# A hypergraph layer whose 512-column rows are turned by VectorE and DMAs instead of TensorE

## The reference

```python
def hypergraph_conv(x, adj, W, b):
    H = (adj != 0).astype(x.dtype)
    w = adj.reshape(N, -1)[:, :C]                  # the first row of adj
    xw = jnp.einsum('ncd,hd->nch', x, W)
    Dn = jnp.einsum('nce,ne->nc', H, w)
    Dn = jnp.where(Dn > 0, 1.0 / Dn, 0.0)
    Be = H.sum(axis=1)
    Be = jnp.where(Be > 0, 1.0 / Be, 0.0)
    m = Be[:, :, None] * jnp.einsum('nce,nch->neh', H, xw)
    out = Dn[:, :, None] * jnp.einsum('nce,neh->nch', H, m)
    return out + b

h = jax.nn.relu(hypergraph_conv(x, adj, W1, b1))   # 512 columns
h = layer_norm(h, gamma, beta)
y = hypergraph_conv(h, adj, W2, b2)
return y + x
```

## Time and profile before

| | us |
|---|---|
| median of three runs | 2948.34 |
| the profiled execution | 2946.47 |
| its span, first to last instruction | 2944.7 |
| PE busy | 2819.0 |
| DVE busy | 1853.9 |
| ACT busy | 1485.6 |
| POOL busy | 723.1 |

### The profile page before, as it was taken

One profiled execution on the slowest core, in us unless ns is written; L12 is line 12 of the kernel. 1 busy time (PEld: TensorE's weight loads), 2 busy tenths in 40 slices (PEclk: granted clock), 3 DMA queues, 4 the chain that ended last, 5 costly groups with the idle time before them and its releaser, 6 DMA issues.

```text
span 2944.7 us, 61858 instructions
## 1 busy us (share of the span) xinstructions
PE 2819.0 (96%) x21760; PEld 2239.6 (76%) x21760; DVE 1853.9 (63%) x3994; ACT 1485.6 (50%) x2761; POOL 723.1 (25%) x1305
## 2 busy tenths in 40 slices
PE   8989999899998999989999999999999999999999
PEld 7777787787877878778687786877868778687786
DVE  3787427874288742887428864398643886439862
ACT  2883318833288332873228732387223872238622
POOL 0342003420034201342013420134101441014410
PEclk9999999999999999999999999999999999999999
DMA  5562215623166130661316613156122661126600
GB/s 177 186 196 93 91 61 194 200 81 113 47 202 209 57 135 35 204 216 42 131 50 196 214 50 118 67 189 219 57 96 79 190 219 64 74 82 198 199 8 15
DMA packets 210505, 371.89 MB, mean 126 GB/s; under 512 B 23312, under 2 KB 136336, under 8 KB 210192
## 3 DMA queue, kind: packets, MB, share of 16 engines
q1 hardware_dynamic: 208656, 363.59, 37.3%
q0 software_dynamic: 1536, 4.20, 0.4%
HBM read 220.64 MB, written 92.54 MB: 106 GB/s over the span
## 4 chain that ended last, share of the span: by engine, by line
PE 71%; DVE 15%; issue 7%; POOL 3%; ACT 2%; SPq 1%; DVEq 1%; DMA 0%; POOLq 0%; ACTq 0%
PE ps L1266 37%; PE ps L1432 7%; PE ps L1552 7%; PE ps L1489 7%; PE ps L1454 6%; PE ps L1627 4%; DVE junk L973 3%; POOL H L696 2%; DVE Z L929 2%; DVE stats L747 1%; SPq L507 1%; DVE h L989 1%; DVE dn L982 1%; DVE h L1007 1%; DVE Zx L929 1%
## 5 line engine op out<-in xcount | busy, mean ns | idle before, releaser
L1432 PE MATMUL ps<-kS,qS 128*128 128x512 f32 x1024 | 380.3, 454 | 88.3 <-DVE nm L929 85.9
L929 DVE CUSTOM_DVE_ANT_0 Z<-ps,adjN 128x1024 f32<-128x1024 f32 x328 | 393.7, 1207 | 36.1 <-PE ps L1432 34.8
L1187 ACT ACTIVATE Z<-Z,nm 128x1024 f32<-128x1024 f32 x328 | 378.2, 1156 | 18.0 <-POOL nm L684 16.9
L696 POOL TENSOR_SCALAR H<-adjN 128x128 fp32r<-128x128 f32 (+1 forms) x456 | 317.5, 697 | 0.0
L1177 ACT ACTIVATE PTa<-ps 128x512 f32<-128x512 f32 x464 | 253.9, 597 | 63.6 <-PE ps L1454 62.4
L1432 PEld LDWEIGHTS ps<-kS,qS 128*128 128x128 f32 x1024 | 161.0, 189 | 163.3 <-DVE nm L929 134.5
L684 POOL TENSOR_TENSOR nm<-nm,minus 128x1 f32<-128x1 f32 x512 | 98.2, 192 | 582.9 <-DVE nm L929 582.6
L1454 PEld LDWEIGHTS ps<-ident,Z 128*128 128x128 f32 x1792 | 204.7, 140 | 39.1 <-issue 14.8
L1454 PE MATMUL ps<-ident,Z 128*128 128x128 f32 x1792 | 233.4, 274 | 0.6
L929 DVE CUSTOM_DVE_ANT_0 Zx<-ps,adjN 128x1024 f32<-128x1024 f32 x184 | 221.0, 1204 | 8.0 <-PE ps L1432 6.9
L1266 PE MATMUL ps<-mh,adjT 128*128 128x256 f32 x1024 | 223.6, 379 | 0.8 <-issue 0.8
(11 more groups left out here) (192 smaller groups left out, 6202.7 us busy)
## 6 DMA issues: line engine op xcount, KB each, us to landing
blocks_kept<-blocks_in SPq DMA_DIRECT2D x160, 512.0 KB, 3.0
blocks_even<-blocks_kept SPq DMA_DIRECT2D x288, 128.0 KB, 3.4
adjT<-adjT_in SPq DMA_DIRECT2D x8, 4096.0 KB, 14.2
adjN<-adj_in SPq DMA_DIRECT2D x8, 4096.0 KB, 17.3
PTb<-blocks_kept SPq DMA_DIRECT2D x224, 128.0 KB, 3.5
PTz<-blocks_kept SPq DMA_DIRECT2D x128, 128.0 KB, 3.3
adjT<-adjT_in SPq DMA_DIRECT2D x8, 2048.0 KB, 7.7
qS<-qhi SPq DMA_DIRECT2D x112, 128.0 KB, 2.1
```

What stands on the lines that cost most here:

```text
L696: done = pool.tensor_scalar(H[:, t, of], adjN[:, t, of], 0.0, 0.0, ALU.is_equal, ALU.is_equal)
L929: dve.tensor_tensor_reduce(Z_of(u), ps[:, 2 * (u % 2):2 * (u % 2) + 2].rearrange("p a n -> p (a n)"), adjN[:, u // HEADS], SCORE_SCALE, LO ...
L1187: act.activation(Z_of(u), Z_of(u), ACT.Exp, bias=nm[:, u:u + 1], accum_out=sm[:, HEADS * (u // HEADS) + place(u):HEADS * (u // HEADS) + pl ...
L1432: mm = pe.matmul(ps[:, 2 * (u % 2) + s], qS[:, hd, rows(t)], kS[:, hd, half(s)], start=True, stop=True)
```

## The change

After the change DVE turns each tile of h2 in 32x32 blocks into a buffer `h2_turned` (two tiles), as soon as relu is done and ahead of the statistics. SP writes the buffer to DRAM (`h2_kept`); after each second tile it waits for both writes and reads both tiles back into `h2T` with four DMAs, one for each 32 partitions. Each DMA has 8 pieces of 512 bytes on each of 32 partitions. `h2T` has a new layout: the four blocks of columns of a row lie next to each other, so the elements of one stationary tile for x2 stand 16 bytes apart, and DVE writes its blocks with the same step. PE's transposes and ACT's copies go. The subtraction that makes Ul moves from DVE to POOL, between the scales of the third and the fourth norm.

```diff
@@ signals
-        h2T_ps = signal("h2T_ps", FT * NH)
-        h2Ts = signal("h2Ts", FT * NH)
+        h2_blocks = signal("h2_blocks", NT)
+        h2_out = [signal(f"h2_out{n}", 16 * (NT // 2)) for n in range(2)]
+        h2T_in = [signal(f"h2T_in{n}", 16 * QUADS) for n in range(NT // 2)]
@@ SP, after the loads of the weights
+                for t in range(NT):
+                    sp.wait_ge(*h2_blocks(b, t + 1))
+                    stand(sp, waited_sp)
+                    sp.dma_start(h2_kept[t], h2_turned[:, t % 2]).then_inc(h2_out[t % 2].sem, 16)
+                    if t % 2:
+                        for n in range(2):
+                            sp.wait_ge(*h2_out[n](b, 16 * (t // 2 + 1)))
+                            stand(sp, waited_sp)
+                        for to in range(QUADS):
+                            sp.dma_start(h2T[SQ * to:SQ * (to + 1), t - 1:t + 1].rearrange("p t (a q) f -> p (t a) (q f)", q=SQ),
+                                         h2_kept[t - 1:t + 1].rearrange("t (a p) c n -> p c (t a) n", p=SQ)[:, to]).then_inc(h2T_in[t // 2].sem, 16)
@@ POOL, batch()
                 norm_scale(b, 3)
+                for t in range(NT):
+                    pool.wait_ge(*x2h(b, t + 1))
+                    pool.tensor_tensor(Ul[:, t], h[:, t, 0:D], Uh[:, t].bitcast(F32), ALU.subtract).then_inc(x2s.sem, 1)
                 norm_scale(b, 4)
@@ DVE, the loop over y
                     if t:
                         dve.wait_ge(*yrelu(b, t))
+                        if t > 2:
+                            dve.wait_ge(*h2_out[(t - 1) % 2](b, 16 * ((t - 1) // 2)))
+                        dve.transpose(h2_turned[:, (t - 1) % 2].rearrange("p a (q c) -> p c a q", q=SQ), h2[:, t - 1]).then_inc(h2_blocks.sem, 1)
                         statistics(b, 3, t - 1, h2[:, t - 1])
@@ DVE, the loop over x2
-                    dve.wait_ge(*x2h(b, t + 1))
-                    dve.tensor_tensor(Ul[:, t], h[:, t, 0:D], Uh[:, t].bitcast(F32), ALU.subtract).then_inc(x2s.sem, 1)
@@ ACT
-                def copy_h2T(s):
...
-                    if t == H2T_AT - 1:
-                        copy_h2T(0)
...
-                    if t == TPH - 2:
-                        copy_h2T(1)
@@ PE
-                def transpose_h2(s):
...
-                    if t == H2T_AT:
-                        transpose_h2(0)
...
-                    if t == TPH - 2:
-                        transpose_h2(1)
-                    if t % TPH == 0:
-                        pe.wait_ge(*h2Ts(b, FT * (t // TPH + 1)))
+                    if t % 2 == 0:
+                        pe.wait_ge(*h2T_in[t // 2](b, 16 * QUADS))
...
-                    product(ps[:, t % 4, 0:D], [(h2T[:, f, rows(t)], W2g[:, f]) for f in range(FT)]).then_inc(x2_ps.sem, 1)
+                    product(ps[:, t % 4, 0:D], [(h2T[:, t, :, f], W2g[:, f]) for f in range(FT)]).then_inc(x2_ps.sem, 1)
```

More of the change, by code:

```diff
@@ L186, in build_program @@
              ("PTb", [P, PTS - PTA - 1, NT, P], F32), ("rs", [P, HEADS, HD], F32), ("Rs", [P, GROUPS, P], F32)],
-            [("h2", [P, NT, HID], F32), ("h2T", [P, FT, N], F32)],
+            [("h2", [P, NT, HID], F32), ("h2T", [P, NT, QUADS * SQ, FT], F32)],
             [("hh", [P, NT, HW], F32R), ("hl", [P, NT, D], F32R), ("wB", [P, N], F32), ("junk", [P, N], F32)],
@@ L191, in build_program @@
             [("padc", [P, NH, NT, HALF], F32), ("shiftB", [P, 2, D], F32),
-             ("b1B", [P, HID], F32)],
+             ("b1B", [P, HID], F32), ("h2_turned", [P, 2, QUADS, FT * SQ], F32)],
         )
@@ L200, in build_program @@
         P3, E3 = p3
-        _, shiftB, b1B = p2c
+        _, shiftB, b1B, h2_turned = p2c
+        h2_kept = nc.dram_tensor("h2_kept", [NT, P, QUADS, FT * SQ], F32, kind="Internal").ap()
         (r1, r2, r3) = region(
@@ L445, in weighed_before @@
             return GROUPS * (u // HEADS - 1) + place(u) // HPG + 1
-        H2T_AT = TPH + 2
         EARLY_EDGES = (5, 6, 4)
```

## The result

The changed kernel takes **3012.06 us** (median of four runs, 3010.18 to 3015.33) against 2948.2 before on the same chip: ratio 1.0215, 95% interval 1.0203 to 1.0228. The forecast was 2992, range 2955 to 3042: slower, as forecast, by 64 us instead of 44. The profiled executions differ by 66.1 us (span 3010.8 against 2944.7), 8.3 us a pass.

What follows compares the result with a forecast made beforehand. PE, busy 96%, bounds the kernel; after the change SP's round trip, 5.2 us per two tiles, does. Each pass loses 5.8 less 0.34, so 5.5 us; eight passes, 44 us, on 2946.5, plus 1.9, give 2992 us, range 2955 to 3042.

Steps and rivals of the forecast that it cites:

- the 0.34 us of the earlier trace: Edge sums: their wait for DVE's last x2 tiles goes, as no subtraction is left between those tiles; 0.34 us less a pass.
- PE needs 16 x 0.216 = 3.46 us for two tiles: x2 products: PE's time for each pair of tiles, 3.46 us, below SP's step of 5.2 us.
- Rival 2: PE slows while it waits for x2's reads: first pair alone costs nothing, all four pairs give 3077 us; chance 4%.
- Rival 1: x2's weight loads, slowed by the 16-byte step from 190 ns to 380, cost 5 us more a pass: 3032 us; chance 15%.
- I take no penalty: DVE's new block transposes: writing with a 16-byte step costs nothing extra, so each takes 0.70 us.
- SP's steps of 5.2, 5.45 and 5.2 us: SP's round trip per two tiles (four reads, two writes, waits): 5.2 us, the second step with 0.25 us of DVE's.
- Rival 3: The trip is short and PE's saving real: 13 us gained, 2935 us; chance of a gain 4%, of a tie 5%.
- DVE alone would pace: Were a pair in 4.0 us after its transpose, DVE would set the pace and the fourth pair start 1.3 us earlier.
- GpSimd's subtractions: Eight subtractions moved to GpSimd, about 0.65 us each, hidden behind the edge sums; without that cover they would cost 1 us.

Runs made afterwards that it cites:

- e7: The changed kernel with a few matmuls without use ahead of each pair's wait, so that PE does not stand still: 3000.43 us.
- e1: The changed kernel without the 16-byte step in DVE's blocks and in x2's weights (product mixes columns, only its time is of use): 3000.63 us.
- e2: The changed kernel with only the x2 weights lying side by side, DVE still writing with the 16-byte step (product not the reference's): 3010.94 us.
- e3: The changed kernel with only DVE writing in runs of 32 elements, the weights still with the 16-byte step (product not the reference's): 3006.44 us.
- e5: The changed kernel with x2 multiplying untransposed h2 without waiting for the trip, which still runs (not the reference's product): 2985.38 us.
- e6: e5 with DVE also writing its blocks in runs of 32 elements (not the reference's product): 2970.04 us.
- e4: The kernel before, with nothing but the subtraction moved to GpSimd: 2946.99 us, ratio 0.9996.
- e9: e8 with e1's two edits and matmuls without use, (3, 1, 1, 1), before the pairs: 2977.29 us, ratio 1.0097.
- e8: The changed kernel with the reads issued by ScalarE's queue, so that SP has only writes: 2993.81 us.

## Why the prediction was right, and its size too small

The mechanism was right: the new wait is the trip from DVE to DRAM and back, SP's round trip paces it, and nothing behind the edge sums gives the delay back but the 0.34 us of the earlier trace rows (from the sums to the next pass's y it is 331.7 us in the fourth pass, before 332.2). Its steps for the fourth pass, forecast and trace, in us from the start of y:

| | forecast | after |
|---|---|---|
| first, second reads issued | 13.4, 18.6 | 13.36, 18.83 |
| third, fourth reads issued | 24.0, 29.2 | 24.35, 30.01 |
| first pair starts | 18.6 | 17.92 |
| fourth pair starts | 34.5 | 35.28 |
| sums over edges start | 37.7 | 40.56 |

- **The step that failed: "PE needs 16 x 0.216 = 3.46 us for two tiles"**, used for the last pair as 3.27 until the sums. It takes 5.28: 2.0 of the 2.8 us that are missing in the fourth pass. 1.5 are the lower clock; e7 gives back 1.45. The other 0.5 it takes at the full clock as well: the last pair of e7 and of the changed kernel's first pass needs 3.75 instead of 3.27. With loads of 190 ns such a pair needs 3.37 (e1), so 0.4 of it is the weights' step and 0.1 the start behind a wait.
- **Rival 2** had the right mechanism with too few cases: the first pair alone (costs nothing) or all four (3077). The trace shows a third: the clock also falls behind the gap ahead of the *last* pair, and nothing is left there to hide it. I had put the later gaps at 1.7 us; the last is 2.45. The Trainium skill ("TensorE: Matmul & The Clock Gate", HAM oscillation — how this bites in real kernels) describes a low clock after each DMA wait that is longer than the work ahead of it. The traces of this case agree in part: 0.76 in the window of the last pair against 1.00 where e7 fills the gaps, but 1.00 behind the gap of 1.39, and in the last pair of two passes; and the work ahead of the last gap, 4.11 us, is longer than the gap.
- **Rival 1**, loads slowed by the step: 329 ns instead of the 380 supposed, but they do not set the step of PE: 0.233 us against 0.216 at the full clock (0.44 only for the first step behind a wait), not 0.38. e2 shows no gain that can be told without it.
- **"I take no penalty" for DVE's step of 16 bytes** was wrong: 1.11 us, not 0.70. The setup's rows couldn't show it: 27 ns over 24 more columns of another operation, from which I took a rate for a transpose of 512. Per column it is (1110 - 165)/512 = 1.85 ns with the step and (706 - 165)/512 = 1.06 without. In the sum it was covered, by luck, by two terms that erred the other way: writes that run alone landed in 2.0 us, not 2.6, and the first four reads were in, and PE off, after 4.56, not 5.25. So the first reads went out on time. Behind them SP's steps pace the pairs, and so e3 gives 5.6 us, not the 15.3 that lie between e5 and e6. The Trainium skill ("SBUF — State Buffer", Door 1: The DMA port swizzle) says that each access which crosses to a new 16-byte line pays. Here the transposes (1.11 us against 0.71) and the loads (329 ns against 190) agree with it, where I had let stand against it.
- **SP's steps of 5.2, 5.45 and 5.2 us** measured 5.47, 5.52 and 5.66: in the first two the odd write goes out late, behind DVE's slower transpose; in the last both go out at once and the second lands after 3.1 us, not 2.6. That is the other 0.8 us a pass. The last reads take the 5.27 us until PE starts that were forecast as 5.25, but that is luck: the others take 4.38 to 4.56, and the last ones have a cost of their own, below.
- **Rival 3** was priced wrongly, which the result hides. I wrote that with a short trip "DVE alone would pace" and 13 us would be gained. e5 and e6 show 2985 and 2970, both slower than before. I had not seen that x2's fifth tile needs a bank that DVE empties only behind its longer loop. By my own forecast of that loop (transpose 7 ends at 1371.65, y+23.2, its statistics about 1 us later: y+24.2) the fifth tile would have started near y+25.4 and the sums, after e6's 6.8 us for four tiles, near y+32.2: a tie at best.
- GpSimd's subtractions took 0.68 us (forecast 0.65) and are hidden, as e4 shows.

So PE's 36 us of transposes are gone, and no run cashes them: e6, whose PE waits for no trip and pays no step, is 20 us slower than before. The step of DVE's blocks adds 15 (e5, where the clock also falls in eight passes instead of four), and PE's wait for the trip with the weights' step 27 (the changed kernel). Between e9 and e6 stand 7 us. e6's own loss is not shown to be unavoidable: 2.2 us a pass are DVE's wait for its two buffers, and in four passes the clock falls. Without both it would be a tie, by the estimate at e6; a run with more buffers would have to show it.

Open in part: why the last four reads take 5.27 us from issue to PE's start when the first take 4.56 and the third 4.38. Among them falls one packet of another queue (q8), one of instructions, and the rate then stays at 9 to 26 GB/s for eight slices, 1.4 us. The DMA part of 1404 to 1411:

```profile
GB/s 176 12 0 0 0 0 0 0 0 0 32 164 257 281 199 246 287 144 301 263 237 281 196 85 26 9 9 9 12 15 20 18 0 0 0 0 0 0 0 0
...
q8 instruction: 1, 0.02, 1.0%
```

No experiment was made for it, but the traces tie the two together. In the changed kernel a q8 packet of instructions falls among the last four reads of all eight passes, and these are in 5.1 to 5.3 us after the first is issued; the 24 other groups of four have none and are in after 4.3 to 4.4. In e7, with more matmuls in PE's program, the packet falls at the start of the third four in seven passes: those are in after 4.8 to 4.9, and the last four after 4.3 to 4.4. e7's DMA part of 1394 to 1400, the third four:

```profile
q8 instruction: 1, 0.02, 1.3%
```

So some 0.9 us a pass (5.2 less 4.35), an estimated 7 of the 64 us, goes with that packet; how it holds the reads up stays open.

## What to carry to other kernels

Work taken off the busiest engine is worth something only if the engine that takes it over isn't the next in line: follow where its own later work (here the evacuation that frees PSUM banks) now starts, before pricing the transfer. For a queue that waits, reads and writes in order, add up its round trip per step; reads on another queue were worth 18 us here, half of it by a shorter gap that left PE's clock up. And look at the last piece ahead of the next stage: where an earlier piece runs at the lower clock, the wait behind it hides that; behind the last piece no wait is left to hide it. Gains that were measured one by one may be the same gain twice: here e7 and e8 both take away the slow last pair.

## What the runs showed of the hardware that I had not expected

- A step of 16 bytes between written elements makes DVE's 128x512 block transpose 1.11 us instead of 0.71; read as weights, a 128x128 load takes 329 ns instead of 190, while the step of the matmuls at the full clock grew only from 0.216 to 0.233 us.
- In the fourth pass PE's clock fell behind gaps of 3.25 and 2.45 us and not behind that of 1.39 between them (the window 1402 to 1409 has 1.00). But it stayed up behind gaps of 2.38 and 2.32 in the first and the last pass, and behind 3.04 in e6's fourth pass, where it fell in e5's. Over the whole run its mean is 0.991, and 0.999 in e7, which fills the gaps.
- A 256 KB write landed in 2.0 us alone; of two issued 0.46 us apart the first took 2.8 and the second 2.9 (e3, the writes of 1384.36).
- Four reads of 128 KB on SP's queue were in after 4.3 to 4.4 us, and after 5.1 to 5.3 where one packet of instructions on another queue fell among them.
